# Changes at the ends and starts of stages: sixteen-row head stores with separate sums, a new order of the last projection stores, and the first loads of attention on two queues

## What is computed

```python
x = x + _L0_attn_ref(_layernorm(x), Wq, bq, Wk, bk, Wv, bv, Wp, bp)   # window attention, projection
x = x + _L0_ffn_ref(_layernorm(x), gate_w, w_up, w_down, ...)         # experts
x = x + _L1_attn_ref(_layernorm(x), Wq, bq, Wk, bk, Wv, bv)           # block-sparse attention
x = x + _L1_ffn_ref(_layernorm(x), weight, alpha, bias)               # ternary weights
# in each attention: softmax(q k^T * scale) v, per head
```

## Time and profile before

| | us |
|---|---|
| runs, median (lowest to highest) | 2714.09 (2711.36 to 2715.87) |
| the profiled execution | 2722.96 |
| its span in the trace | 2721.2 |
| busy: TensorE, VectorE, ScalarE, GpSimd | 2236.0, 1889.8, 1691.1, 1072.8 |
| p0 ends and a0 starts, in the span | 172.77 |
| a0 ends and stage_combine starts | 819.52 |
| p1 ends and a1 starts | 1849.95 |
| a1 ends and stage_close starts | 2546.7 |

### The profile page before, as it was taken

The page is one execution under the profiler, slowest core; times in us unless marked ns, Lnnn a source line. Parts: engine busy times, 40 slices in busy tenths (PEclk is TensorE's granted clock), DMA queues, the critical chain, the costliest instruction groups (busy, mean ns, idle before and its releaser), DMA issues. The chain is left out here.

```text
span 2721.2 us, 71969 instructions
## 1 busy us (share of the span) xinstructions
PE 2236.0 (82%) x25421; PEld 1285.8 (47%) x25421; DVE 1889.8 (69%) x5617; ACT 1691.1 (62%) x3876; POOL 1072.8 (39%) x1325
## 2 busy tenths in 40 slices
PE   7957888888877588859999994992999999998464
PEld 4622333333324376748888883551343434343243
DVE  4538888888826577644545455765999999996285
ACT  6935777777762355514545444770788888889243
POOL 3523444444447677746666662540000000000165
PEclk9977999999988799979999997995899999999687
DMA  7442222222203266645554344763122222221296
GB/s 231 182 145 57 75 75 80 77 76 74 80 21 123 68 164 187 168 127 118 135 129 102 91 89 133 256 228 106 45 74 70 75 69 75 70 74 35 62 180 152
DMA packets 393755, 297.94 MB, mean 109 GB/s; under 512 B 258592, under 2 KB 326944, under 8 KB 393408
## 3 DMA queue, kind: packets, MB, share of 16 engines
q1 hardware_dynamic: 375904, 249.02, 34.6%
q0 software_dynamic: 12960, 35.60, 3.8%
q10 hardware_dynamic: 4544, 8.72, 1.1%
HBM read 133.53 MB, written 123.69 MB: 95 GB/s over the span
## 5 line engine op out<-in xcount | busy, mean ns | idle before, releaser
L701 ACT ACTIVATE a_pr<-a_pst 128x384 f32<-128x384 f32 (+3 forms) x2176 | 934.5, 482 | 226.4 <-PE a_pst L736 189.1
L649 DVE TENSOR_REDUCE a_mx<-a_psc 128x1 f32<-128x384 f32 (+2 forms) x1152 | 587.9, 566 | 45.3 <-PE a_psc L736 35.6
L802 PE MATMUL a_po<-a_pr,a_ve 128*17 128x128 f32 (+3 forms) x10496 | 565.3, 303 | 2.2 <-ACT a_pr L701 1.3
L644 DVE CUSTOM_DVE_ANT_0 a_cut<-a_psc,row_mask 128x384 bf16<-128x384 f32 (+1 forms) x1024 | 497.3, 522 | 88.3 <-PE a_psc L736 41.7
L736 PE MATMUL a_psc<-a_ke,a_qe 52*128 52x128 f16 (+5 forms) x3072 | 375.4, 289 | 154.3 <-DVE a_mx L644 53.5
L623 POOL TENSOR_SCALAR_AFFINE_SELECT a_pr<-a_pr 128x512 f32<-128x512 f32 x448 | 275.0, 634 | 366.7 <-ACT a_pr L701 366.7
L736 PE MATMUL a_pst<-a_qe,a_ke 53*128 53x128 f16 (+5 forms) x3072 | 368.1, 284 | 41.6 <-ACT a_pr L701 19.8
L736 PEld LDWEIGHTS a_psc<-a_ke,a_qe 52*128 52x128 f16 (+1 forms) x3072 | 123.6, 94 | 351.1 <-DVE a_mx L644 187.4
L736 PEld LDWEIGHTS a_pst<-a_qe,a_ke 53*128 53x128 f16 (+1 forms) x3072 | 113.7, 94 | 356.7 <-ACT a_pr L701 323.5
L802 PEld LDWEIGHTS a_po<-a_pr,a_ve 128*17 128x17 f32 x10496 | 194.1, 96 | 185.6 <-issue 130.5
L861 POOL MEMSET t_spread<- 128x2048 f32 x1 | 1.8, 1804 | 706.6 <-POOLq L464 706.6
(11 more groups left out here) (233 smaller groups left out, 4264.2 us busy)
## 6 DMA issues: line engine op xcount, KB each, us to landing
a_qe<-qx SPq DMA_DIRECT2D x384, 64.0 KB, 2.8
a_ke<-kx SPq DMA_DIRECT2D x384, 64.0 KB, 2.8
vx<-p_vst SPq DMA_DIRECT2D x32, 544.0 KB, 3.2
a_ve<-vx SPq DMA_DIRECT2D x64, 272.0 KB, 3.2
ox<-a_ost SPq DMA_DIRECT2D x256, 68.0 KB
qx<-p_stg SPq DMA_DIRECT2D x64, 256.0 KB, 2.8
kx<-p_stg SPq DMA_DIRECT2D x64, 256.0 KB, 3.1
x_res<-x SPq DMA_DIRECT2D x16, 512.0 KB, 9.9
```

The source lines that it names most:

```text
L644: dve.tensor_tensor_reduce(out=cut[:, n % 4, 0:width], in0=psc[(u * n_s + n) % RING][:, 0:width], in1=row_mask[:, at:at + width], scale=1. ...
L649: dve.tensor_reduce(out.unsqueeze(1), psc[(u * n_s + n) % RING][:, 0:width], AXX, ALU.max)\
L701: act.activation(pr[s % SLOTS][:, h // 2, h % 2, 0:width], pst[prob_slot(u, n) % RING][:, 0:width], ACT.Exp, scale=scale).then_inc(p_ready, 1)
L802: last = pe.matmul(po[h][32 * a:32 * a + VW, tok % CH:tok % CH + w], ve[g][:, t, a * VW:(a + 1) * VW], pr[s % SLOTS][:, a // 2, a % 2, col ...
```

## The change

- In stage_project the last batch's q and k parts are stored before the last chunk's values, and every batch's parts are stored as they become ready, with a wait for each m.
- In stage_attend each head is stored as 16 rows, and the four sums of a unit go with a fifth DMA to a new tensor, sums. The first unit's loads are split: six on SyncE's queue, six on ScalarE's ahead of the constant rows. The semaphore for those rows is split by group, and TensorE waits for a group's rows with the first scores of the group.
- Shares loads all sums with one DMA, and in stage_close ScalarE waits for them after it has issued the heads of the first two chunks.
- ox has 16 rows per head.

```diff
             def store_qk(b):
-                sp.wait_ge(qk_lo, 8 * b + 8)
                 for m in range(4):
+                    sp.wait_ge(qk_lo, 8 * b + 4 + m + 1)
...
+                if c == NC - 1:
+                    store_qk(c // 2)
                 store_v(c)
-                if c % 2:
+                if c % 2 and c < NC - 1:
                     store_qk(c // 2)
...
-        rows_set, po_set = sem("rows_set"), sem("po_set")
+        rows_set, po_set = [sem(f"rows_set{g}") for g in range(HG)], sem("po_set")
...
+        def load_half(dma, g, b, par):
+
+            for term, (q_part, k_part) in enumerate(((0, 0), (0, 1), (1, 0))):
+                r = slice(par * 64 + term * DH, par * 64 + (term + 1) * DH)
+                dma.dma_start(qe[g][r, :, :], qx[q_part, 2 * g + par, :, :, bass.ds(b * N, N)]).then_inc(qk_loaded[g], 16)
+                dma.dma_start(ke[g][r, :, :], kx[k_part, 2 * g + par, :, :, bass.ds(b * N, N)]).then_inc(qk_loaded[g], 16)
...
                 for h in range(4):
-                    sp.dma_start(ox[g, h * VW:(h + 1) * VW, bass.ds(b * N, N)],
-                                 ost[g % 2][32 * h:32 * h + VW, :, :]).then_inc(o_stored[g % 2], 16)
+                    sp.dma_start(ox[4 * g + h, :, bass.ds(b * N, N)],
+                                 ost[g % 2][32 * h:32 * h + DH, :, :]).then_inc(o_stored[g % 2], 16)
+                sp.dma_start(sums[b * H + 4 * g:b * H + 4 * g + 4, :], ost[g % 2][DH:P:32, :, :]).then_inc(o_stored[g % 2], 16)
 
             def start():
-                for g in range(3):
+                load_half(sp, 0, 0, 0)
+                for g in range(1, 3):
                     load_qk(g, 0)
...
             def start():
+                load_half(act, 0, 0, 1)
                 for g in range(HG):
                     for par in range(2):
...
                 if n == 0:
+                    if b == 0:
+                        pe.wait_ge(rows_set[g], (1 if const_rows is None else 3) * 2 * 16)
                     pe.wait_ge(qk_loaded[g], b * (N_LOAD * 16) + N_LOAD * 16)
...
-                pe.wait_ge(rows_set, HG * (1 if const_rows is None else 3) * 2 * 16)
...
     def load(self, dma):
-        for b in range(B):
-            dma.dma_start(self.sums[b * H:(b + 1) * H, :], self.ox[:, DH, b * N:(b + 1) * N]).then_inc(self.loaded, 16)
+        dma.dma_start(self.sums[:, :], self.sums_in).then_inc(self.loaded, 16)
...
     def heads(self, c, e):
-        return self.ox[e * 8:(e + 1) * 8, 0:DH, c * CH:(c + 1) * CH]
+        return self.ox[e * 8:(e + 1) * 8, :, c * CH:(c + 1) * CH]
...
             for c in range(OR):
+                if c == 2:
+                    act.wait_ge(shares.loaded, 16)
                 load(c)
...
-    ox = nc.dram_tensor("ox", [HG, 4 * VW, T], F32, kind="Internal").ap()
+    ox = nc.dram_tensor("ox", [H, DH, T], F32, kind="Internal").ap()
+    sums = nc.dram_tensor("sums", [B * H, N], F32, kind="Internal").ap()
```

More of the change, by code:

```diff
@@ L444, in block_rows, with stage_attend @@
     return np.repeat(rows[:, :, None, :], 2, axis=2)
-def stage_attend(nc, epoch, tag, jobs, scale, row_mask, const_rows, mrow, ident16, qx, kx, vx, ox):
+def stage_attend(nc, epoch, tag, jobs, scale, row_mask, const_rows, mrow, ident16, qx, kx, vx, ox, sums):
     nj = len(jobs)
@@ L493, in stage_attend @@
         N_LOAD = 12
+        N_STORE = 5
         N_CUT = sum(len(m) for _, _, m in jobs)
@@ L551, in load_qk @@
             def load_qk(g, b):
-                tok = b * N
                 for par in range(2):
[L554 to L559, removed]
+                    load_half(sp, g, b, par)
             def load_v(g, b):
@@ L609, in end @@
                 for s in range(2):
-                    sp.wait_ge(o_stored[s], UNITS // 2 * 64)
+                    sp.wait_ge(o_stored[s], UNITS // 2 * N_STORE * 16)
             streams(sp, start, step, end)
@@ L683, in copy_out @@
                 u = unit(g, b)
-                after(act, o_stored[g % 2], b * 128 + (g // 2) * 64)
+                after(act, o_stored[g % 2], (2 * b + g // 2) * N_STORE * 16)
                 act.wait_ge(p_used, u * nj + last_of[h] + 1)
@@ L719, in start @@
                         if const_rows is not None:
-                            act.dma_start(qe[g][r, :, :], const_rows[0]).then_inc(rows_set, 16)
-                            act.dma_start(ke[g][r, :, :], const_rows[1]).then_inc(rows_set, 16)
-                        act.dma_start(ke[g][par * 64 + KS:par * 64 + KR, :, :], mrow[:, :].unsqueeze(1).to_broadcast([1, 2, N])).then_inc(rows_set, 16)
+                            act.dma_start(qe[g][r, :, :], const_rows[0]).then_inc(rows_set[g], 16)
+                            act.dma_start(ke[g][r, :, :], const_rows[1]).then_inc(rows_set[g], 16)
+                        act.dma_start(ke[g][par * 64 + KS:par * 64 + KR, :, :], mrow[:, :].unsqueeze(1).to_broadcast([1, 2, N])).then_inc(rows_set[g], 16)
                 turn(0, 0)
@@ L844, with __init__ @@
 class Shares:
-    def __init__(self, nc, ctx, sem, tag, ox):
-        self.ox = ox.rearrange("g (h w) t -> (g h) w t", w=VW)
+    def __init__(self, nc, ctx, sem, tag, ox, sums_in):
+        self.ox, self.sums_in = ox, sums_in
         self.sums = ctx.enter_context(nc.sbuf_tensor(f"{tag}_sums", [P, N], F32))
@@ L870, in invert @@
         cols = slice(half * CH, half * CH + CH)
-        dve.wait_ge(self.loaded, B * 16)
+        dve.wait_ge(self.loaded, 16)
         dve.reciprocal(self.rec[:, cols], self.sums[:, cols]).then_inc(self.ready, 1)
@@ L882, in heads, with stage_combine @@
     def heads(self, c, e):
-        return self.ox[e * 8:(e + 1) * 8, 0:DH, c * CH:(c + 1) * CH]
-def stage_combine(nc, epoch, tag, x_res, mean, rstd, ox, wp_in, bp_in):
+        return self.ox[e * 8:(e + 1) * 8, :, c * CH:(c + 1) * CH]
+def stage_combine(nc, epoch, tag, x_res, mean, rstd, ox, sums, wp_in, bp_in):
     with ExitStack() as ctx:
@@ L903, in stage_combine @@
         ah, al = sb("ah", [P, AR, EC, CH], F16), sb("al", [P, AR, EC, CH], F16)
-        shares = Shares(nc, ctx, sem, tag, ox)
+        shares = Shares(nc, ctx, sem, tag, ox, sums)
         stats = Stats(nc, ctx, sem, tag, mean, rstd)
@@ L1698, in _, with stage_close @@
             down(NJ - 1, older)
-def stage_close(nc, epoch, tag, x_res, ident, ox, w_in, alpha_in, bias_in, out):
+def stage_close(nc, epoch, tag, x_res, ident, ox, sums, w_in, alpha_in, bias_in, out):
     with ExitStack() as ctx:
@@ L2015, in build @@
             stage_attend(nc, epoch, "a0", window_jobs(), 1.0 / (QS * QS * D ** 0.5), row_mask, None, mrow, ident16,
-                         qx, kx, vx, ox)
-            stage_combine(nc, epoch, "c0", x_res, mean, rstd, ox, l0_wp, l0_bp)
+                         qx, kx, vx, ox, sums)
+            stage_combine(nc, epoch, "c0", x_res, mean, rstd, ox, sums, l0_wp, l0_bp)
             def kept(n, shape, dt):
@@ L2029, in build @@
             stage_attend(nc, epoch, "a1", block_jobs(), 1.0 / (QS * QS * DH ** 0.5), None, brows, mrow, ident16,
-                         qx, kx, vx, ox)
-            stage_close(nc, epoch, "t", x_res, ident, ox, tern_w, tern_alpha, tern_bias, out)
+                         qx, kx, vx, ox, sums)
+            stage_close(nc, epoch, "t", x_res, ident, ox, sums, tern_w, tern_alpha, tern_bias, out)
 def kernel(**inputs):
```

## The result

The changed kernel takes 2666.03 us in the median of four runs (2663.94 to 2668.1), the kernel before 2714.98 us beside it. The ratio is 0.9821 with an interval of 0.9804 to 0.9838, a gain of 49 us. Forecast were 2673.9 us and a gain of 40; the range of 2664 to 2688 holds the median, 2 us above its lower end. The profiled span is 2666.3 us.

A forecast was written before the change was run, and what follows sets the result against it. The prediction saw engines waiting for each other within the attention body and the money at the joints between stages. Eight gains summed to 40.2 us, off the median of 2714.09 giving 2673.9 us, range 2664 to 2688.

The forecast's parts named there:

- The eight terms: Gains at joints and stage starts in both layers: 4.3, 4.3, 1.6, 5.5, 8.2, 8.5, 1.8 and 6.0 us, together 40.2 us.
- Part 1: Joint of projection to attention: q and k parts stored one by one, values last, 4.3 us sooner in each layer.
- the case of my upper bound: End of the projection: stores go out at GpSimd's 1.26 us per pair, gaining 5.0 us per layer.
- Part 2: Start of attention: first unit's loads on two queues, row semaphores per group, 1.6 us in layer 0, 5.5 in layer 1.
- Part 3: Joint after attention: heads stored as 16 rows, sums apart, 8.2 us in layer 0 and 8.5 in layer 1.
- The fifth store's bounds: End of attention: the four-row store's issue takes 0.4 to 0.7 us; joint gains bounded by 7.4 and 9.0 us each.
- Part 4: Start of the stages after attention: all sums in one load, 1.8 us in layer 0 and 6.0 in layer 1.
- the taking of turns with the heads in layer 1: Start of stage_close: sums alternate with heads' loads on the engines, through after 2.6 us, 5.2 with fixed cost and issue.
- my bound without any contention: Start of stage_close: the sums' load unhindered by the heads takes 3.5 us, a gain of 7.7 us.
- (a): Attention starts: the second queue brings nothing or less, 8.4 us less gain than forecast, 2682 us; chance 0.10.
- (b): Joints after attention: 16 rows still go through one engine, 16.7 us of gain vanish, 2691 us; chance 0.08.
- (c): Attention bodies: the fifth store makes SyncE's queue the bound of each of 64 units, slower, 2763 us; chance 0.03.

The follow-up runs named there:

- padded17: The changed kernel with one dead row behind each head in ox and 17 rows per head stored again, fifth store kept: 2687.08 us, ratio 0.9901.
- split16_1: The kernel before with each 17-row store cut into one of 16 rows and one of 1 row, same tensor and layout: 2695.74 us, ratio 0.9925.
- padded: The changed kernel with one dead row behind each head in ox, so heads' rows are unevenly spaced, 16 rows still stored: 2673.92 us, ratio 0.9839.

## Why the prediction was right, and where it was short

The eight terms were 40.2 us on paper and 42.4 in the traces, most of them by the mechanism that was told; where they were not, it is said below. That the median fell into the range is in part luck: some 6 us came from a place for which the sum has no term, and the range, wide for other reasons, had 2 us to spare.

**Part 1: 4.3 and 4.3 us forecast, 4.7 and 4.7 in the traces**, 8.1 in the timed runs of the part alone. The order acts as told. The mis-sized term is SyncE's issue: I took 0.7 us per store from rows in which the wire was full (all sixteen DMA engines busy). Spread out by GpSimd's pace, four took 2.11 us, so the stores went out at that pace, the case of my upper bound: eight in 4.7 us and not 5.6. Against it, the value store took 4.2 us to the next stage and not 3.6. What my sum of issue times does not say is that the data set the end: eight stores of 256 KB and one of 544 KB are 2.6 MB, the wire is full at 370 GB/s from 158 to 165 us, they need 7.2 us at that rate, and the stage starts about a microsecond after the wire has run empty. By this trace the gain comes from starting that stream sooner; no run tests whether a faster issue would bring more. That the split waits cost earlier batches nothing I took from the earlier trace rows, which cover the attention and not the projection; the lengths of p0 (159.6 to 161.5 us in all kernels with the new order, 160.5 to 163.1 with the old) bear it out.

**Part 2: 1.6 and 5.5 us forecast, 0.9 and 4.5 in the traces, 1.1 and 5.0 between the means of all kernels with the new beginning and the old.** The wait went where I put it, to the mask rows. The term of 3.5 us from a row's last issue to TensorE was short for a queue that carries loads too. The second row of group 0 was issued at about 171.15 (8 rows in 5.67 us from 170.44), and TensorE started 4.2 us later; in a1 the sixth was issued at 1829.94, and TensorE started 4.3 us later. The timed runs do not show the gain of this part.

**Part 3: 8.2 and 8.5 us forecast, 9.0 and 9.7 in the traces.** Cause and place are shown by padded17 and split16_1. The term that failed is the 3.6 us from the last issue to the next stage. I carried it over from the projection, whose 2 MB of stores fill the wire. Behind small transfers it was 2.6 us (802.92 to 805.55). The fifth store's bounds were right, 0.51 us of issue.

**Part 4: 1.8 and 6.0 us forecast, 1.9 and 7.0 in the traces.** The term that failed is the taking of turns with the heads in layer 1, priced at 5.2 us with all that goes with it: 4.2 it was with heads on sixteen engines, and with eight, the case that I had priced, 3.5 in padded and 3.4 in padded17. That is my bound without any contention. The part as a whole is worth 8 us in the traces and some 10 in the timed runs. The wait in it is worth nothing.

**What was missed.** I weighed the rule of engine counts on the stores and never turned it on the loads, though I had read the earlier trace rows as eight engines. The change makes the rows of the heads evenly spaced, and the loads take all sixteen. That is 5 to 6 us in stage_close and the most of what the sum lacked: 42.4 + 5.9 is 48.3, against 49.0 measured (the first two from traces, the last from timed runs, so that they meet to a microsecond is no proof). In the profiled pair the span fell by 54.9 us, since the profile of before was high in p0 and in the routing (163.1 and 399.4 us, where the other kernels show 159.6 to 161.5 and 393.6 to 397.2); I do not count that difference as the change's.

**The rivals.** (a) fell as a loss: with one queue layer 0 was slower, by 1.0 to 1.3 us. The Trainium skill's rule ("DMA: Bandwidth & Descriptors", "Issuing engines are not separate DMA queues") is that a second issuing engine saves issue time alone, usually little; I had put that case at nothing and my own at 1.6 us, and the runs lie between. (b) fell with split16_1. (c) fell too: the body of a0 takes 622.4 us in the mean of the eight kernels with the fifth store and 622.6 in the four without, split16_1 with its four extra ones among them.

## What to carry to other kernels

Look at the DMA share between stages: 0.06 of sixteen engines is one engine, and with 16 rows and the odd one sent apart the joint here was 5.0 us long and not 14.1. When a layout changes, ask of every transfer that reads or writes it, and not only of the one the change is about, over how many engines it will run. Issue the last stores as their parts become ready, so that their data are on the way before the stage's work ends. And compare a single start or stage with other traces of the same code before reading half a microsecond out of it.

## What was not expected

With twice the engines for the heads' loads other transfers were faster: DMA transposes on SyncE's queue, which the change does not touch, landed in 3.0 instead of 4.0 us in the median. And from the last issue to the start of the next stage it took 3.6 and 4.2 us behind a full wire, 2.6 us behind a store of 16 KB and 2.0 us behind one of 4 KB (split16_1, 805.84 to 807.85).
